# Quantised weights made in the place they stay, with four of twelve low halves taken from TensorE's PSUM

## What is computed

```python
# layer 1: a Mamba-2 block (8 heads of 64, state 128)
zxbcdt = u @ in_proj_kernel                      # 256 -> 1288
xBC = silu(causal depthwise conv1d(xBC, 4 taps))
dt  = softplus(dt + dt_bias);  A = -exp(A_log)
Y   = chunked scan (decay matrices, states)  + x * D
y   = rmsnorm(Y * silu(z)) * norm_weight @ out_proj_kernel
# layer 2: a gated MLP whose weights are 4-bit codes with a scale for each block of 32
W    = LUT[code] * scale                         # gate, up: 2048 x 256; down: 256 x 2048
out  = (gelu(x1 @ gate.T) * (x1 @ up.T)) @ down.T
```

## Time and profile before

| | |
|---|---|
| median of 3 runs | 1014.07 us (1013.44 to 1014.91) |
| the profiled execution | 1015.02 us, span 1013.3 us |
| PE busy | 922.1 us, 91% of the span |
| DVE busy | 792.3 us, 78% |
| ACT busy | 599.6 us, 59% |
| POOL busy | 340.2 us, 34% |
| chain that ended last | PE 73%, DVE 14%, ACT 6%, issue 4% |

### The profile page before, as it was taken

The page is one execution under the profiler, slowest core; times in us unless marked ns, Lnnn a source line. Parts: engine busy times, 40 slices in busy tenths (PEclk is TensorE's granted clock), DMA queues, the critical chain, the costliest instruction groups (busy, mean ns, idle before and its releaser), DMA issues.

```text
span 1013.3 us, 17021 instructions
## 1 busy us (share of the span) xinstructions
PE 922.1 (91%) x6048; PEld 809.1 (80%) x6048; DVE 792.3 (78%) x2079; ACT 599.6 (59%) x1014; POOL 340.2 (34%) x346
## 2 busy tenths in 40 slices
...
GB/s 150 79 60 65 1 4 8 12 11 1 12 1 32 1 11 1 12 22 1 12 1 32 2 11 1 11 23 1 11 1 32 1 12 1 1 22 1 1 21 11
DMA packets 13828, 17.64 MB, mean 17 GB/s; under 512 B 1712, under 2 KB 10416, under 8 KB 13744
## 3 DMA queue, kind: packets, MB, share of 16 engines
...
q10 hardware_dynamic: 864, 0.03, 0.1%
...
## 4 chain that ended last, share of the span: by engine, by line
PE 73%; DVE 14%; ACT 6%; issue 4%; DMA 1%; POOL 1%; ACTq 0%; DVEq 0%; POOLq 0%
PE fb L1088 28%; PE db L1088 14%; PE mb L1088 14%; DVE xc L892 6%; PE mb L1198 5%; PE mb L1189 3%; PE mb L1207 2%; PE mb L1181 2%; PE mb L1213 1%; ACT L704 1%; DVE stage L1051 1%; ACT lmat L637 1%; DMA dsk<-in_d_skip 1%; ACT xc L657 1%; DVE raw L883 1%
## 5 line engine op out<-in xcount | busy, mean ns | idle before, releaser
L554 POOL TENSOR_TENSOR hl<-hid,hl 128x512 fp32r<-128x512 f32 (+1 forms) x144 | 169.6, 1179 | 416.1 <-ACT hl L711 415.9
L1088 PE MATMUL fb<-x1t,wg 128*128 128x512 f32 (+1 forms) x864 | 214.5, 384 | 5.4 <-DVE x1t L994 5.3
L1088 PE MATMUL db<-wd,hl 128*128 128x256 f32 x1536 | 217.7, 290 | 1.6 <-POOL hl L554 1.5
L1088 PEld LDWEIGHTS db<-wd,hl 128*128 128x128 f32 x1536 | 198.7, 190 | 16.6 <-issue 9.6
L1088 PE MATMUL fb<-x1t,wu 128*128 128x512 f32 (+1 forms) x864 | 205.6, 374 | 3.5 <-ACT hid L704 3.5
L1088 PEld LDWEIGHTS fb<-x1t,wu 128*128 128x128 f32 x864 | 152.5, 191 | 37.2 <-ACT hid L704 6.5
L1088 PEld LDWEIGHTS fb<-x1t,wg 128*128 128x128 f32 x864 | 145.3, 191 | 30.5 <-DVE x1t L994 6.5
L1000 DVE TENSOR_TENSOR hid<-fb,hid 128x512 f32<-128x512 f32 (+1 forms) x144 | 90.2, 627 | 75.5 <-PE fb L1088 67.1
L711 ACT ACTIVATE hl<-hid 128x512 fp32r<-128x512 f32 (+1 forms) x144 | 83.4, 580 | 102.0 <-DVE hid L1000 75.4
L892 DVE SCALAR_TENSOR_TENSOR xc<-raw,cw,xc 128x256 f32<-128x256 f32 x288 | 132.9, 528 | 9.2 <-ACT xc L657 8.0
L704 ACT ACTIVATE hid<-fb 128x512 f32<-128x512 f32 (+1 forms) x144 | 78.3, 548 | 81.1 <-PE fb L1088 77.3
...
## 6 DMA issues: line engine op xcount, KB each, us to landing
...
wo_raw<-in_out_proj SPq DMA_DIRECT2D x1, 512.0 KB, 10.8
...
cb<-in_conv_b ACTq DMA_DIRECT2D x1, 3.0 KB, 2.8
```

The source lines that it names most:

```text
L554: pool.tensor_tensor(hl[:, hs, n % 2, 1, :], hid[:, hs, n % 2, :], hl[:, hs, n % 2, 0, :].bitcast(F32), ALU.subtract).then_inc(s["lo"], 1)
L1088: last = pe.matmul(ps, lhs(a, k), rhs(b, k), start=start and n == 0, stop=stop and n == len(todo) - 1, skip_group_check=check)
```

## The change

- The packed words, the scales and the product of a piece no longer pass through the buffers `words` and `stage`. They lie in the bytes where that piece's high and low part will stay (`wg_raw`, `wu_raw`, `wd_raw` are the float32 names of `wg`, `wu`, `wd`): words where half of the high part goes, scales in the other half, spread codes and then the product where the low part goes. Each piece has semaphores of its own.
- SP therefore waits for nothing and issues all 24 loads of words and scales one behind the other.
- For the pieces 6, 8, 10 and 11 (`LO_ON_PE`) VectorE makes no subtraction. TensorE adds in a PSUM bank the product by the identity (float32) and the high part by minus the identity (`minus`, fp32r), and ScalarE copies the bank to the low part; a step `lo:q` does this for the two halves e = 0 and e = 1, both by way of the bank `db[0]`. ScalarE makes `minus` once from the identity.
- The table `FIRST` is re-ordered on all four engines; `ORDER` and `LAST` stay.

```diff
+LO_ON_PE = (6, 8, 10, 11)
+LO_IN_TWO_BANKS = tuple(q for q in LO_ON_PE if q < 3)
...
-        xtr:3 out:2 yo:3 yd:3 st:3 yt:3 out:3 z:0> z:1> ip:0> ip:1> x1t:1 ip:2> z:2> cs:0> gu:0 ct:0> seg:0>
...
+        yt:2 xtr:3 lo:8 out:2 yo:3 yd:3 lo:10 st:3 yt:3 lo:11 out:3 z:0> z:1> ip:0> ip:1> x1t:1 ip:2> z:2> cs:0>
...
-                if q >= 2:
-                    sp.wait_ge(piece_f32, q - 1)
-                sp.dma_start(words[w][:], packed[mat, :, c0:c0 + PIECE]).then_inc(words_loaded[w], 16)
-                if q == 2:
-                    sp.wait_ge(wo_ready, 1)
-                if q >= 3:
-                    sp.wait_ge(piece_lo[r], q // 3)
-                sp.dma_start(stage[r][:, 1, :], scales[mat, :, c0:c0 + PIECE].unsqueeze(1)
-                             .broadcast_to([8, SBLK // 2, PIECE])).then_inc(scales_loaded[r], 16)
+                sp.dma_start(words(q), packed[mat, :, c0:c0 + PIECE]).then_inc(words_loaded[q], 16)
+                sp.dma_start(scale_of(q), scales[mat, :, c0:c0 + PIECE].unsqueeze(1)
+                             .broadcast_to([8, SBLK // 2, PIECE])).then_inc(scales_loaded[q], 16)
...
+            def lo(i, par, q):
+
+                for e in range(2):
+                    act.wait_ge(lo_psum, lo_uses().index((q, e)) + 1)
+                    act.activation(piece(q, 1)[:, e], lo_bank(q, e)[:].rearrange("p (g n) -> p g n", n=DM), ACT.Copy).then_inc(lo_read if e == 0 else piece_lo[q], 1)
...
             def dl(i, par, q):
 
-                mat, c0, r = q % MATS, q // MATS * PIECE, q % 3
                 dve.wait_ge(piece_hi, q + 1)
-                dve.tensor_tensor(weight_piece(mat, 1, c0), staged(r), weight_piece(mat, 0, c0).bitcast(F32),
-                                  ALU.subtract).then_inc(piece_lo[r], 1)
+                dve.tensor_tensor(piece(q, 1), product(q), piece(q, 0).bitcast(F32),
+                                  ALU.subtract).then_inc(piece_lo[q], 1)
...
+            def lo(i, par, q):
...
+                for e in range(2):
...
+                    if e == 0:
+                        pe.wait_ge(piece_f32, q + 1)
+                    ps = lo_bank(q, e)[:].rearrange("p (g n) -> p g n", n=DM)
+                    pe.matmul(ps, ident[:], product(q)[:, e], start=True, stop=False)
+                    if e == 0:
+                        pe.wait_ge(piece_hi, q + 1)
+                    pe.matmul(ps, minus[:], piece(q, 0)[:, e], start=False, stop=True).then_inc(lo_psum, 1)
```

More of the change, by code:

```diff
@@ L127 @@
[L127 to L135 removed]
+        xt:1 ip:3 z:3 z:4 ip:4 ip:5 cs:1 z:5 ct:1 seg:4 seg:5 seg:6 gb:1 seg:7 yo:2 xtr:2 st:2 xt:0> lo:6 yd:2
```

195 lines of the change are left out of this document (107 added, 88 removed).

## The result

The changed kernel takes 1020.08 us (median of 4 runs, 1019.88 to 1020.98), the kernel before in the same session 1013.76 (1013.40 to 1014.91). The ratio is 1.0057, 95% interval 1.0043 to 1.0071: slower by 5.8 us, between 4.4 and 7.2. The forecast was 1012.8, its range ended at 1019.5, and the nearest rival was "PE at the half clock" with 1020.3. The profiled execution took 1020.03, span 1018.3.

What follows compares the result with a forecast made beforehand. It took VectorE to set the pace while weights are made, ScalarE in the second stretch, PE alone from about 200 us. Terms 1.0 - 0.7 - 1.6 = -1.3 gave 1013.7 profiled, 1012.8 median, range 1006 to 1019.5.

Steps and rivals of the forecast that it cites:

- PE at the half clock: Rival for the scan: `lo` 5.6, `yd` 3.4, `out` 2.9, `stats2:3` 8.5 late, sum +6.2, 1020.3 us; chance 0.14.
- I take 4.2: Price of one `lo` step on PE in us, by the middle row, between bounds of 3.3 and 5.6.
- So the 10.6 are spent: `stats2:3` is 1.0 late: End of the scan: the gain of 10.6 at `gb` is used up, `stats2:3` at 94.7 where 93.7 was.
- the 113 us: Sign: the later iterations, where PE alone is the chain of waits, keep their length of 113 us.
- The sign against the `lo` price: VectorE busy over 95% from 52 to 90 would show the `lo` price wrong.
- The start: ScalarE copies the input projection at once, so `xn_split:1` starts at 23.1, not 28.3: gain 5.2, bounds 0 and 5.2.
- the third rival: At the start, the full queue delays output projection or constants by 5, everything behind 5.2 later: 1018.0 us; chance 0.09.
- To `gb`: From `xn_split:1` to `gb`: less work on VectorE and ScalarE, `gb` near 47.4 instead of 58.04, gain 10.6.
- The scan: From `xdt:2` at 52.2 to `stats2:3` at 94.7, with four `lo` steps on PE and four low parts saved on VectorE.
- Behind them: From `stats2:3` to the end of `conv:2`: VectorE does one `scale` (1.2) less, partly lost to later gates: -0.7.
- The second stretch: Three table loads gone where ScalarE bounds, 3.8 in all, `decay_sums:7` gaining 2.5: -1.6, bounds 0 and 3.8.
- full clock: Rival for the scan: `lo` 3.3, `yd` 1.9, `out` 1.7, gain 4.7, sum -7.0, 1007.1 us; chance 0.29.

Runs made afterwards that it cites:

- e5: Changed kernel plus 35 dummy products on PE where it would only wait, low parts still through one bank: 1014.11 us, ratio 0.9986 to the kernel before.
- e3: Changed kernel with the two halves of each low part in two banks, so no wait for ScalarE's copy between: 1011.86 us, ratio 0.9983 to the kernel before.
- e12: Changed kernel with `minus` ahead of `wi_split` on ScalarE, so the first table load comes earlier: 1019.62 us, ratio 1.0068 to the kernel before.
- e10: Pieces in place, low parts on VectorE, several moved later, `ln2:2` drawn ahead, 38 dummy products on PE: 1010.68 us, ratio 0.9963 to the kernel before.
- e7: Kernel before with only the new order of the second stretch, from `gu:8` on, on all four engines: 1014.26 us, ratio 0.9988 to the kernel before.
- e11: Changed kernel with two banks per low part and dummy products in PE's waits, none between the halves: 1011.75 us, ratio 0.9979 to the kernel before.
- e6: Kernel before with only the new order of the start on ScalarE and VectorE, old staging buffers kept: 1012.23 us, ratio 0.9972 to the kernel before.
- e1: Changed kernel without `lo` steps, the four subtractions back on VectorE at about the same places: 1012.71 us, ratio 0.9989 to the kernel before.
- e2: Changed kernel without `lo` steps, the four subtractions on VectorE but later, where it was idle before: 1011.82 us, ratio 0.9981 to the kernel before.

## Why the prediction was wrong

**The step that failed: "I take 4.2"**, the price of one `lo`, with `yd` 2.6 and `out` 2.3, and what the walk makes of it: "So the 10.6 are spent: `stats2:3` is 1.0 late". Measured: 4.4, 5.7, 5.0 and 5.0, with `yd:2` 1.9 and the two `out` 2.4 and 2.8, and `stats2:3` 6.6 late. The mechanism was right at every joint: the low parts stand in front of `yd:2`, `out:2`, `st:3` and `out:3`, VectorE runs out of work, and the 10 us won by `gb` are used up by `stats2:3`. The size was off. I took the middle row because the mean clock of the old stretch was 0.64. But a mean clock isn't a price: it is a mixture of full and half, and the new steps fell into the half, since PE waits for VectorE ahead of three of them and for ScalarE in the middle of each. e5 and e3 show that this is the cause: with PE busy in the waits, or without the pause, the same chain falls to 3.5 and 2.6 where the clock is full, and 7.2 and 7.5 us come back. The bounds were sound (3.3 at full clock: 3.5; 5.6 at half: 5.7), and so was the point from which the rival decides, "a `lo` of about 5 us". Its chance of 0.14 was too small.

Of the signs that were to show it, the start, `xdt:2` (53.0), the pause in each pair, the six table loads and the 113 us came. VectorE's 3 us of idle time ahead of `ydiag:2` (1.6) and `stats2:3` between 93 and 96 (100.3) did not. The sign against the `lo` price, VectorE busy over 95% from 52 to 90, could only have shown a cheaper `lo`: VectorE was busy 80% there, and the `lo` was dearer.

The other terms, in their order:

- *The start*, "gain 5.2": measured 3.8. The miss is VectorE's `wo_raw` step of 2.72, into which POOL's step was brought by the table load behind the wait for `wi`, which the forecast let run ahead of it; e12 gets it back. VectorE's `wo_raw` began at 12.97, and the constants kept nobody waiting: the third rival, a delay of 5 us, is out. The full queue may not be free, though. The slower half of `wi` landed 5.3 to 5.6 us after its issue in the three traces with the old loads and 5.4 to 7.8 in the eleven with the 24 at once (5.9 in the change; the 7.8 made the late start of e10). No run tells the queue from chance. The Trainium skill (DMA: Bandwidth & Descriptors, "Queues, rings and completion order") says that each DMA engine takes turns between the queues it has work for; the output projection, 10.7 us after its issue for 10.8 before, shows no price of that here.
- *To `gb`*, 10.6 by forecast: 9.5. Behind `xn_split:1` the step was even slightly too pessimistic (5.7 won, 5.4 foreseen).
- *The scan*: 42.5 us by forecast from `xdt:2` to `stats2:3`, 47.3 measured. Of the 4.8 the `lo` steps are 3.3 (20.1 against 16.8), and `scale:10` beside POOL another 1.3, a cost that I didn't see. The old trace shows the effect: VectorE's 16-column subtraction at 16.25 takes 2.31 beside POOL's 2.96 and the `dq` at 66.98 1.64 instead of 0.69 beside `yoff`. I never looked for the pair.
- *Behind them*, -0.7: from `stats2:3` (+6.6) to `gate:3>` (+6.4) it is -0.2, so half a microsecond of it did not come.
- *The second stretch*, -1.6: 0.8 in place, 1.2 alone (e7; 1.0 in its trace). The six table loads are there, and `decay_sums:7` gains 2.4 of the 2.5 foreseen; PE, near its half clock ahead of `xtr:2>`, took the rest.
- *The rivals*: full clock, 1007.1, is refuted for this kernel, and e11 shows that it was too hopeful besides. At full clock from 56 to 92 us, in two banks, the kernel takes 1011.8, since VectorE is still busy 35.4 of the 41.8 us from `gb` to `stats2:3`. The half clock, 1020.3, is 0.2 off in the sum by luck: its walk had `stats2:3` at 102.2, later than the 100.3 measured, and a start that was 1.4 better, and the gains of 0.7 and 1.6 behind the scan were 0.2 and 0.8.

On the rule that the prediction weighed against this change: the rows first. In two of the four low parts the product behind the pause in one bank ran at 2.07 where the one ahead of it had 1.32, and without the pause the clock of the stretch rose from 0.72 to 0.81. The Trainium skill (TensorE: Matmul & The Clock Gate, "A second HAM failure mode: psum-queue depth-cycling") says that short idle times as banks are cycled let the clock swing; the trace agrees, and I should have given that case more than one chance in seven.

The whole change, taken apart by the runs: the start -2.8 (e6), the second stretch -1.2 (e7), the four low parts on PE +6.9 (the change against e1). Together these would be +2.9, and the change is at +5.8. The 2.9 that remain (an estimate from the intervals of e1, e6 and e7 gives 1.2 to 4.6) are the pieces in place and the middle order, as e1 shows: with both re-orderings and without `lo` it reaches -1.1 and not -4.0. The traces tell where they went. Up to `stats2:3` the two stand together (90.67 in e1, 90.78 in e6), though e1 was 6.7 us ahead at `gb`. That lead was mostly VectorE's work put off from ahead of `gb` to behind it: VectorE is busy 38.7 us from `gb` to `stats2:3` in e1 and 33.0 in e6 (1.4 of the difference are steps held up longer beside POOL). Where VectorE is the limit this isn't a gain but a loan. From `stats2:3` to `gate:3>` e1 then needs 58.0 us, e6 and the kernel before 56.0. From `gate:3>` to the first wide `gu` e1 wins 1.3 (53.9 for 55.2). So e1's second stretch did come, and 2.0 us had been lost ahead of it. There e1 has `dl:11` ahead of `ln2:3`, for which PE waits; e2 and the change, which don't, need 56.8 and 55.8. That this place of `dl:11` is the reason is likely, but no run moves it alone.
